# Routing stage of an adaLN MoE kernel: row forming and two biases on GpSimd, and a new order of all engines between the scan and the experts

## What is computed

```python
kv = h @ W_KV; k, v = split(kv)
params, _ = scan(step, (W1, b1, W2, b2), (k, v))      # p - LR * grad of mean((mlp(p, k_t) - v_t) ** 2)
attn = silu(q @ W1 + b1) @ W2 + b2                     # q = h @ W_Q
x = x + ga * attn
h = layernorm(x) * (1 + cb) + sb
logits = h @ w_router.T; probs = softmax(logits); vals, idx = top_k(probs, 2)
hs  = gelu(h @ Ws1.T + bs1);          acc = hs @ Ws2.T + bs2            # shared expert
h_e = gelu(h @ W1[e].T + b1[e]);      y_e = h_e @ W2[e].T + b2[e]       # d_ff = 512
x = x + gb * SCALE * (acc + sum_e gates[e] * y_e)
```

## Time and profile before

| | us |
|---|---|
| median of 3 runs | 676.57 (676.39 to 676.61) |
| the profiled execution | 677.3 |
| its span, first to last instruction | 675.5 |
| PE busy in the span | 601.8 (89%) |
| DVE busy | 427.0 (63%) |
| ACT busy | 330.0 (49%) |
| POOL busy | 353.3 (52%) |

### The profile page before, as it was taken

The page is one execution under the profiler, slowest core; times in us unless marked ns, Lnnn a source line. Parts: engine busy times, 40 slices in busy tenths (PEclk is TensorE's granted clock), DMA queues, the critical chain, the costliest instruction groups (busy, mean ns, idle before and its releaser), DMA issues. The chain is left out here.

```text
span 675.5 us, 14646 instructions
## 1 busy us (share of the span) xinstructions
PE 601.8 (89%) x4334; PEld 525.1 (78%) x4334; DVE 427.0 (63%) x1745; ACT 330.0 (49%) x1050; POOL 353.3 (52%) x569
## 2 busy tenths in 40 slices
PE   1459999999999999999958876969789999999997
PEld 1338999999999999999844755858577999999972
DVE  2846888888888888888856789543123444544526
ACT  1455666666666666666624756414123434443420
POOL 1025666666666666666611088888662354555520
PEclk9999999999999999999989588879987999999999
DMA  9059910000000000000000016122333577787447
GB/s 207 13 216 413 411 54 1 1 0 0 0 0 0 0 0 0 0 0 0 2 1 1 0 42 216 37 74 60 127 123 114 160 218 236 213 251 222 141 156 241
DMA packets 39668, 66.76 MB, mean 99 GB/s; under 512 B 7394, under 2 KB 26596, under 8 KB 39620
## 3 DMA queue, kind: packets, MB, share of 16 engines
q1 hardware_dynamic: 30948, 54.84, 25.5%
q0 software_dynamic: 4544, 9.45, 3.9%
q10 hardware_dynamic: 4128, 1.91, 1.2%
HBM read 36.25 MB, written 29.92 MB: 98 GB/s over the span
## 5 line engine op out<-in xcount | busy, mean ns | idle before, releaser
L1941 POOL DMA_INDIRECT ys<-yo,dst x78 | 74.7, 958 | 83.8 <-DVE yo L1842 68.1
L1548 ACT ACTIVATE hid<-bank,slab 128x256 f32<-128x256 f32 x156 | 63.2, 471 | 106.5 <-PE bank L1411 77.0
L1930 POOL DMA_INDIRECT xs<-hrow,slot_i x64 | 63.3, 989 | 45.2 <-issue 38.8
L1427 PEld LDWEIGHTS bank<-slab,hid 128*128 128x128 f32 x624 | 79.0, 199 | 4.4 <-DVE yb L1837 1.5
L1427 PE MATMUL bank<-slab,hid 128*128 128x128 f32 x624 | 79.8, 283 | 0.9 <-issue 0.8
L1411 PE MATMUL bank<-hg,slab 128*128 128x256 f32 x312 | 74.7, 383 | 0.4 <-DVE hg L1805 0.4
L1411 PEld LDWEIGHTS bank<-hg,slab 128*128 128x128 f32 x312 | 57.2, 193 | 6.9 <-issue 0.6
L395 PE MATMUL bank<-aH,W2p 128*128 128x128 f32 x192 | 42.4, 303 | 0.1
L395 PE MATMUL bank<-kv,W1b 128*128 128x128 f32 x192 | 41.4, 298 | 0.0
L1837 DVE TENSOR_TENSOR yb<-bank,slab 128x256 f32<-128x256 f32 x39 | 16.6, 424 | 38.2 <-PE bank L1427 30.2
L972 POOL TENSOR_TENSOR nL<-aL,ones 128x128 f32<-128x128 bf16 x32 | 17.7, 552 | 42.7 <-ACT aL L681 42.7
(11 more groups left out here) (339 smaller groups left out, 1896.6 us busy)
## 6 DMA issues: line engine op xcount, KB each, us to landing
slab<-in_slabs_dram SPq DMA_DIRECT2D x39, 578.0 KB
xs<-fill SPq DMA_DIRECT2D x34, 528.0 KB, 6.1
xt<-xs SPq DMA_DIRECT2D x39, 132.0 KB
yg<-ys SPq DMA_DIRECT2D x8, 512.0 KB, 6.5
xr<-in_L_attn_x_dram SPq DMA_DIRECT2D x8, 256.0 KB, 9.1
ys<-yo,dst POOLq DMA_INDIRECT x78
xs<-hrow,slot_i POOLq DMA_INDIRECT x64
out_dram<-xr SPq DMA_DIRECT2D x16, 64.0 KB, 1.8
```

The lines of the kernel that those rows point to most:

```text
L1427: mm = pe.matmul(y[:, s * D:(s + 1) * D], hid[i % 2][:, n, s * P:(s + 1) * P], right, start=(n == 0 and kind == "expert"), stop=(n == FT - ...
L1548: nc.scalar.activation(hid[i % 2][:, n, :], e_half(i, n), ACT.Gelu_apprx_tanh, bias=bias).then_inc(e_x, 1)
L1930: pool.indirect_dma_start(out=xs[:, :], out_offset=bass.IndirectOffsetOnAxis(ap=slot_i[:, i, c:c + 1], axis=0), in_=hrow[:, c, :], in_offs ...
L1941: pool.indirect_dma_start(out=ys[:, :], out_offset=bass.IndirectOffsetOnAxis(ap=dst[r][:, s:s + 1], axis=0), in_=yo[r][:, s, :], in_offset ...
```

## The change

Six things change, all in the tail program.

- `rows(g)` leaves DVE. POOL gets `scale(g)` and `shift(g)` in its place, one instruction of 512 columns each.
- `EARLY` is gone: POOL adds the attention bias for all eight groups, and the six bias matmuls of `result` go.
- The bias of the shared expert, times its gate, becomes a tile `gsb`. POOL adds it to `xr` once a group (`add_shared_bias`). All 16 bias matmuls go, and `post` and `e_post` wait for POOL's add (`xs_ready`).
- The `idle` memsets go. In their place POOL's list has these instructions between dispatched chunks.
- Eight calls on DVE that were `tensor_tensor` or `tensor_scalar` are written as `scalar_tensor_tensor`, with the same shapes. One of them reads a new constant tile `ecol`.
- The order of PE, ACT, DVE and POOL is new: more `up` and `down` lie between the routing steps, and `JOBS` has S13 after E8 and no longer at the end.

```diff
-JOBS += [("shared", n) for n in range(EARLY_SH + 4, N_SH)]
+JOBS += [("shared", n) for n in range(EARLY_SH + 5, N_SH)]
...
-                    if g >= EARLY:
-                        pe.matmul(bank[2 + g % 2][:, :], ones[:, :], diag[:, :].unsqueeze(1).broadcast_to([P, GRP, D]),
-                                  start=True, stop=False, skip_group_check=True)
...
-                    pe.matmul(y[:, 0:SH], ones[0:1, :], bs2row[:, :], start=True, stop=False, skip_group_check=True)
...
                     dve.wait_ge(post_ready, t + 1)
+                    dve.wait_ge(xs_ready, t * SUB // GRP + 1)
                     xc = xr[:, t * SUB:(t + 1) * SUB, :]
-                    dve.tensor_tensor(xc, ysh[t % 2][:, :, :], xc, ALU.add).then_inc(sh_ready, 1)
+                    dve.scalar_tensor_tensor(out=xc, in0=ysh[t % 2][:, :, :], scalar=1.0, in1=xc,
+                                             op0=ALU.mult, op1=ALU.add).then_inc(sh_ready, 1)
...
+                def scale(g):
+                    pool.wait_ge(xn_ready, g + 1)
+                    pool.tensor_tensor(hrow[:, g * GRP:(g + 1) * GRP, 0:D], xn[:, part(g) % 2, (g - PARTS[part(g)][0]) * GRP:(g - PARTS[part(g)][0] + 1) * GRP, :],
+                                       cbrow[:, :].unsqueeze(1).broadcast_to([P, GRP, D]), ALU.mult).then_inc(scaled, 1)
+
+                def shift(g):
+                    pool.wait_ge(scaled, g + 1)
+                    hx = hrow[:, g * GRP:(g + 1) * GRP, 0:D]
+                    pool.tensor_tensor(hx, hx, sbrow[:, :].unsqueeze(1).broadcast_to([P, GRP, D]), ALU.add).then_inc(placed, 1)
+
+                def add_shared_bias(g):
+                    pool.wait_ge(gab_ready, 2)
+                    pool.wait_ge(xn_ready, g + 1)
+                    xg = xr[:, g * GRP:(g + 1) * GRP, :]
+                    pool.tensor_tensor(xg, xg, gsb[:, :].unsqueeze(1).broadcast_to([P, GRP, D]), ALU.add).then_inc(xs_ready, 1)
+
+                def slots_of(k):
                     pool.wait_ge(col_ready, k + 2)
                     pool.wait_ge(gates_ready, 2 * k + 2)
                     pool.wait_ge(slot_ready, k + 1)
+                    pool.wait_ge(placed, PARTS[k][1])
...
-                        if k < 3:
-                            nc.gpsimd.memset(idle[:, :], 0.0).then_inc(paused, 1)
-                            pool.wait_ge(paused, c + 1)
```

More of the change, by code:

```diff
@@ L1438, in _ @@
                 result(1)
[L1439 to L1442, removed]
+                for g in range(2, NG):
+                    hidden(g)
                 result(2)
                 result(3)
-                hidden(6)
-                hidden(7)
                 turn(0)
@@ L1459, in _ @@
                 places(1)
+                down(0)
+                up(1)
                 turn(4)
                 turn(5)
-                down(0)
-                up(1)
-                route(2)
                 down(1)
                 up(2)
+                route(2)
+                down(2)
+                up(3)
                 places(2)
+                down(3)
+                up(4)
                 turn(6)
                 turn(7)
-                down(2)
-                up(3)
+                down(4)
+                up(5)
                 route(3)
-                down(3)
-                up(4)
+                down(5)
+                up(6)
                 places(3)
-                down(4)
-                for t in range(5, EARLY_SH):
+                down(6)
+                for t in range(7, EARLY_SH):
                     up(t)
@@ L1589, in _ @@
                 to_gelu()
-                for t in range(4, EARLY_SH):
+                for t in range(6, EARLY_SH):
                     gelu(t)
@@ L1873, in _ @@
                 choose(1)
+                times_gate(6)
+                times_gate(7)
                 spread(2)
@@ L1944, in _ @@
                 nc.gpsimd.memset(epsc[:, :], EPS).then_inc(eps_ready, 1)
+                nc.gpsimd.memset(ecol[:, :], float(E)).then_inc(ecol_ready, 1)
                 pool.wait_ge(gab_ready, 1)
-                for g in range(EARLY):
+                for g in range(NG):
                     add_bias(g)
-                for k in range(3):
-                    dispatch(k, *chunks(k))
-                c0, c1 = chunks(3)
-                for j in range((c1 - c0) // 2):
-                    scatter(j)
-                    dispatch(3, c0 + 2 * j, c0 + 2 * j + 2)
-                for j in range((c1 - c0) // 2, N_TILES):
+                for g in range(2):
+                    scale(g)
+                    shift(g)
+                    add_shared_bias(g)
+                slots_of(0)
+                dispatch(0, 0, 1)
+                scale(2)
+                dispatch(0, 1, 2)
+                shift(2)
+                dispatch(0, 2, 3)
+                scale(3)
+                dispatch(0, 3, 4)
+                shift(3)
+                dispatch(0, 4, 6)
+                add_shared_bias(2)
+                dispatch(0, 6, 8)
+                add_shared_bias(3)
+                slots_of(1)
+                dispatch(1, 8, 10)
+                scale(4)
+                dispatch(1, 10, 12)
+                shift(4)
+                dispatch(1, 12, 14)
+                scale(5)
+                dispatch(1, 14, 16)
+                shift(5)
+                add_shared_bias(4)
+                slots_of(2)
+                dispatch(2, 16, 18)
+                scale(6)
+                dispatch(2, 18, 20)
+                shift(6)
+                dispatch(2, 20, 22)
+                scale(7)
+                dispatch(2, 22, 24)
+                shift(7)
+                add_shared_bias(5)
+                slots_of(3)
+                scatter(0)
+                dispatch(3, 24, 26)
+                add_shared_bias(6)
+                scatter(1)
+                dispatch(3, 26, 28)
+                add_shared_bias(7)
+                scatter(2)
+                dispatch(3, 28, 30)
+                scatter(3)
+                dispatch(3, 30, 32)
+                for j in range(4, N_TILES):
                     scatter(j)
```

106 lines of the change are left out of this document (51 added, 55 removed).

## The result

The kernel after takes 666.8 us, the kernel before 676.5 in the same set of runs. The ratio is 0.9848, 95% interval 0.9831 to 0.9866. That is 9.7 us less by the medians and 10.3 by the ratio; 667 was predicted, 9.7 less. One of the four executions of the change took 698.1 us at a lower granted clock (0.84, the others have 0.96) and is left out of the ratio. The profiled execution took 666.9 us with a span of 665.1. In it the scan ends 1.1 us earlier than in the execution of before (PE's L1425 begins at 352.42, the same matmul of before at 353.49), so a place of the change compares with one of before, or of the prediction, with 1.1 us added.

The account below looks back on a forecast made before the run. PE's work was taken to count in full behind 510, its waits and POOL's line before. E8 at 511 + 128.5 + 4.5 + 3 = 647, then 13.75 and 5.0: 665.8 against 675.5, -9.7; so 666.9, range 656 to 675.

Parts of the forecast that it names:

- POOL's line: POOL's indirect DMAs from first dispatch to last: 113.2 us against 118.5 measured before, first at 388, last at 501.
- The terms -22.6 and +22.5: On POOL between first and last dispatch: 24 memsets go, -22.6 us; 18 tensor instructions come, +22.5 us.
- PE up to the experts: PE from the scan's end to the first expert tile: sum -13.2 us, the tile at about 450, not 463.4.
- the port: DVE instructions with two SBUF inputs stop for POOL's tensor instructions: PE's `xn` waits grow by 7.5 us.
- the rest of the sum, -20.7: PE ahead of the experts: six L1319 go, 6.1 us; nine L1379, 8.6; the wait for `post`, 6.
- the port takes more: Rival: DVE's chains lose 16 us, not 7.5; experts begin at 459; 671 to 675 us; chance 0.13.
- The slow stretch: PE crawls from 495 during the unbroken DMAs from `scatter(2)` on, losing about 10 us; E8 begins at 511.
- starving of PE's instruction supply: Reading of PE's lost 8.7 and 7.9 us before: runs of indirect DMAs starve it, 9 to 10 us into each.
- no starving: Rival: PE doesn't crawl in the run from `scatter(2)`; E8 begins at 501, time 657 us; chance 0.2.
- the rival of pauses too thin: From 450 to 486, DMA runs of four parted by 1.25 us cost PE 19 us; time 681; chance 0.1.
- Behind E8: PE from E8 to the sum: 128.5 us of tiles, three biases fewer, plus a wait of 4.5 us.
- the cover: Shared tiles behind the last expert tile hid its loads; with less, PE waits 4.5 us, slower clock adds 3.

Follow-up runs that it names:

- free set: A set of runs in which the kernel before took 662.0 or 661.8 us; the change took 655.2 us there, 0.9892.
- E9: Not a run: the expert tile on PE's job list whose rows POOL sends last; fed at 504.80 us in the change in a free set.
- with memsets: Kernel after with POOL's 24 tensor instructions of scale, shift and add_shared_bias as memsets of about the same length: 660.0 us, 0.9974.
- held set: A set of runs in which the kernel before took 676 to 679 us; the change took 666.8 us there, 0.9848.
- the change with pauses: Kernel after with nine memsets of 0.96 us, one behind every chunk and scatter from scatter(2) to scatter(5): 663.1 us, 0.9779.

## Why the prediction was right, and where not

**POOL's line: right.** 112.0 us against 113.2, first dispatch 386.2 (387.2 with the 1.1 added; 388 said), tensor instructions 1.27 (1.25 said). The terms -22.6 and +22.5 did nearly cancel. The second is a little less, since the DMA behind a tensor instruction follows it by 0.17 us and not by 0.30: leaving 18 of them out shortened the line by 20.9, 1.16 each. In a free set the time hangs on this line, as its traces show: E9's feed comes 5.2 to 5.7 us behind the start of the last dispatch in all seven traces, of both kinds, where PE waits for it (499.34 to 504.80 in the change; 499.71 to 505.13; 499.65 to 505.33), and of 24.1 us by which the last dispatch came earlier 22.7 reached E9.

**PE up to the experts: right sum, wrong terms.** The first feed is at 449.5 (450.6 with the 1.1 added; 450 said). But the port, put at +7.5, took about 12 us from PE's readiness (436.1 with memsets against 448.5 with tensor instructions, in free sets), and not as longer `xn` waits, which fell. So the rest of the sum, -20.7, has to be near -25. The two errors cancelled, which is luck. The rule of the Trainium skill, "SBUF — State Buffer", section "Who interferes with whom", that a DVE instruction with two SBUF inputs contends with a GpSimd instruction that reads SBUF and not with one that only writes, agrees with the 907 and 428 ns above. My rival "the port takes more", with 16 us, was nearer to the port's size and wrong about its worth: it is on a path that POOL's line hides.

**The slow stretch: about the right end, wrong name, and not always there.** E8 is at 513.6 (with the 1.1 added) against 511. From E7's `up` to E8's it took 21.1 us in the held trace and 9.0 in the free one of the same kernel: 12.1 lost where the sum had 10, in one stretch from 497 (495 said). The step that failed is "I read this as a starving of PE's instruction supply": what the rows show is that results of PE reach their takers 12 to 18 us late, while signals to PE at the same place come within 0.1. Nor is it as tied to the start of a run as the sum had it: PE began to crawl 12.8 us into this run (484.23 to 497.04), not 9 to 10, and in the kernel before 11 us into the second run (491.26 to 502.4). The run was not unbroken to 511: scatters 6 and later waited for `yo`, since PE was slow itself, and the run ended at 504.2. And I took the effect as a property of the program. It depends on the conditions too: in two of four sets it doesn't occur, in none of their eight traces. Had the change been measured there, 655.2 would have stood against 667: the case that I gave 0.2 as "no starving", and just outside the range of 656 to 675. That the set was of the held kind is luck, and from one trace this couldn't be seen.

**Ahead of it:** PE waited 1.7 and 2.2 us for `hg` at 484 to 491, said were 5 to 6 at 487 to 493; the issue waits that I excluded from 450 to 485 came once, 1.5 us at 474.5 to 476. That one and the 1.7 us at 484 stand beside late results where POOL's runs of four are parted by 1.27 us, so the rival of pauses too thin was right in kind and worth 3.2 us at most, not 19.

**Behind E8: right.** From E8 to the sum it is 131.9 us (128.5 + 4.5 = 133.0 said). The wait ahead of the sum is 3.9 (4.5), the sum 2.0 us longer (3). That the cover costs this is shown by both runs with S13 at the end; that it could be had back for nothing is not, since S13 then leaves a gap at E9.

**The bias matmuls**, taken out alone, bring 6.0 us in a free set, and the whole change 6.8. Three of the 22 stand behind E9, 2.5 us by 0.82 each; for the other 3.5 us the trace of the kernel before in a free set is missing. The new order of the engines between the routing steps was not run by itself. **In a held set** the gain is about 10 us, and parting the DMAs of part 3 alone brought 11 in the kernel before. How much of the 10 us is the shorter slow stretch (16.6 us of PE's time before, 12.1 now) is a reading of traces and not shown; no run in a held set took the bias matmuls alone.

## What to carry to other kernels

An engine that sends rows out one indirect DMA at a time is a line like any other: count its places, and ask of every gain elsewhere whether it reaches that line. 12 us of PE's readiness were worth nothing while POOL's line stood, and 3.7 us on that line counted in full. With the line 24 us shorter PE became the limit, and its earlier start was needed. A stretch in which an engine waits for "issue" isn't explained by that word: look at the engines that take its results, and at how late they begin. When a number comes out right, compare its terms: two of these were off by 4 to 5 us and cancelled. And where the kernel before differs by 2% between sets of runs, compare within a set, and give the forecast two values, not one.

## What the runs showed of the hardware

- Results of PE can reach DVE and ACT late while POOL sends indirect DMAs without a break: 9 us late in the middle of a run, 12 to 18 us at its end, where those left come together within 4 us behind the start of the last DMA. With a memset of 0.96 us behind every two DMAs such waits were absent (up to 472 us in the kernel before; from 487.5 to 521 in the change with pauses) or 1.7 us long (part 3 of the kernel before with its pause). Between runs of four parted by 1.27 us they reached 5 us.
- Whether it occurs is settled per set of runs and not by the program: 698.1 or 632.4 us for one kernel, on two chips; 678.9 or 662.0 us for the kernel before, on one chip, 22 minutes apart. What settles it stays open.
- A dispatch takes its place of 1.26 us in both kinds; POOL's line, 112.0 and 112.2 us, shows no difference between them.
- The next DMA follows a tensor instruction of POOL by 0.17 us, another DMA by 0.30, and a memset whose semaphore POOL waits for by 0.28 to 0.8.
- From the start of the last dispatch to PE's feed of its rows it takes 5.2 to 5.7 us, in seven traces.
- DVE's `xr` + `ysh` of 256 columns takes 428 ns beside memsets of POOL and 907 beside tensor instructions.
